# Graph stage: three batches that have only counts move from the end into the middle of the order

## What is computed

```python
edge_index = jnp.stack([src, dst])
x = _layernorm(x + _L0_gnn_ref(x, edge_weight, L0_gnn_bias, edge_index))   # x @ W.T + bias
x = _layernorm(x + _L1_gnn_ref(x, edge_index, ...))   # attention over the edges
x = _layernorm(x + _L2_gnn_ref(x, edge_index, ...))   # GCN: normalised sum over the edges
x = _layernorm(x + _L3_gnn_ref(x, src, dst, ...))     # two SAGE layers: mean over the edges
...
# L0: a dense matrix made from the edges
W = jnp.zeros((OUTDIM, INDIM)).at[row, col].add(nnz_weight)
```

## Time and profile before

| what | us |
|---|---|
| timed runs, median of 3 | 1513.65 |
| lowest and highest of them | 1513.05 and 1515.47 |
| span of the profiled execution | 1553.5 |
| graph stage in the profiled execution, about | 20.5 to 127.6 |

### The profile page before, as it was taken

The page is one execution under the profiler, slowest core; times in us unless marked ns, Lnnn a source line. Parts: engine busy times, 40 slices in busy tenths (PEclk is TensorE's granted clock), DMA queues, the critical chain, the costliest instruction groups (busy, mean ns, idle before and its releaser), DMA issues.

```text
span 1553.5 us, 17781 instructions
## 1 busy us (share of the span) xinstructions
PE 1433.6 (92%) x6845; PEld 1145.2 (74%) x6845; DVE 783.6 (50%) x1359; ACT 421.9 (27%) x716; POOL 254.4 (16%) x309
## 2 busy tenths in 40 slices
PE   3988999748999989899999999999999999999996
PEld 3876888625666656678888888888888888888884
DVE  6996776517888868754336632221033232411243
ACT  7853222235565545312111100110120001201000
POOL 3000000064666655110000010000000100000000
PEclk9997999969999999999999999999999999999998
DMA  1665344454555644152117552230056544400252
GB/s 46 192 181 189 106 126 116 93 157 150 163 155 153 179 146 130 55 185 85 61 42 240 180 189 85 103 145 1 0 190 219 187 124 147 143 1 0 91 194 95
DMA packets 101988, 195.95 MB, mean 126 GB/s; under 512 B 26856, under 2 KB 61465, under 8 KB 101905
## 3 DMA queue, kind: packets, MB, share of 16 engines
q1 hardware_dynamic: 77434, 121.01, 25.8%
q0 software_dynamic: 22800, 73.61, 13.9%
q10 hardware_dynamic: 1670, 0.21, 0.1%
HBM read 140.86 MB, written 53.92 MB: 125 GB/s over the span
## 4 chain that ended last, share of the span: by engine, by line
PE 56%; DVE 1%; DMA 0%; issue 0%; POOL 0%; DVEq 0%; ACT 0%
PE layers_y_ps L1927 35%; PE layers_y_ps L1948 17%; PE layers_turn_ps L1911 2%; PE layers_up_ps L1894 1%; PE layers_y_ps L1964 1%; DMA x_d<-fetched_x 0%; DVE layers_w_lo L2082 0%; DVE layers_y L2126 0%; PE layers_y_ps L1972 0%; DVE layers_y L597 0%; DVE layers_ln_stats L591 0%; PE layers_turn_ps L1882 0%; DVE layers_parts_lo L2099 0%; DVEq L592 0%; PE layers_y_ps L1882 0%
## 5 line engine op out<-in xcount | busy, mean ns | idle before, releaser
L1948 PE MATMUL layers_y_ps<-layers_parts_hi,layers_counts 128*128 128x512 f32 x464 | 143.6, 391 | 0.0
L1948 PE MATMUL layers_y_ps<-layers_parts_lo,layers_counts 128*128 128x512 f32 x464 | 143.3, 390 | 0.0
L1927 PE MATMUL layers_y_ps<-layers_w_hi,layers_parts_hi 128*128 128x512 f32 x400 | 126.0, 396 | 0.0
L1927 PE MATMUL layers_y_ps<-layers_w_lo,layers_parts_hi 128*128 128x512 f32 x400 | 123.6, 390 | 0.0
L1927 PE MATMUL layers_y_ps<-layers_w_hi,layers_parts_lo 128*128 128x512 f32 x400 | 123.5, 390 | 0.0
L509 POOL DMA_INDIRECT attention_got<-xl_d,attention_src x104 | 106.5, 1024 | 63.1 <-DVE attention_weighted L1537 31.3
L1948 PEld LDWEIGHTS layers_y_ps<-layers_parts_lo,layers_counts 128*128 128x128 f32 x464 | 87.1, 188 | 18.7
L1948 PEld LDWEIGHTS layers_y_ps<-layers_parts_hi,layers_counts 128*128 128x128 f32 x464 | 86.9, 188 | 18.9
L1353 PE MATMUL attention_mix_ps<-attention_weighted,attention_hot 128*110 128x260 f32 x368 | 95.7, 384 | 3.7 <-DVE attention_weighted L1537 3.7
L1320 PE MATMUL attention_row_ps<-attention_bent,edges_att_rows 128*128 128x512 f32 x184 | 97.1, 611 | 0.0
L2099 DVE SCALAR_TENSOR_TENSOR layers_parts_lo<-layers_y_ps,layers_parts_hi 128x1024 fp32r<-128x1024 f32 x16 | 19.6, 1225 | 147.5 <-ACT layers_parts_hi L2043 147.5
(11 more groups left out here) (341 smaller groups left out, 2783.4 us busy)
## 6 DMA issues: line engine op xcount, KB each, us to landing
layers_counts<-counts_d SPq DMA_DIRECT2D x30, 640.0 KB, 4.0
layers_rest<-x_d SPq DMA_DIRECT2D x23, 512.0 KB, 4.1
self_d<-layers_y POOLq DMA_DIRECT2D x20, 512.0 KB, 6.0
x_d<-layers_y POOLq DMA_DIRECT2D x19, 512.0 KB, 2.9
fetched_x<-x_d SPq DMA_DIRECT2D x17, 512.0 KB, 3.7
fetched_raw<-in_L_gnn_W_self POOLq DMA_DIRECT2D x16, 512.0 KB, 5.9
fetched_raw<-in_L_gnn_W_neigh POOLq DMA_DIRECT2D x16, 512.0 KB, 9.0
heads_dst_wide<-in_dst_held SPq DMA_DIRECT2D x13, 512.0 KB, 4.0
```

The costliest lines, as they stand in the source:

```text
L1927: last = nc.tensor.matmul(y_ps[n % 2][:, a:a + HALF], rows_in[t][:, k * P:(k + 1) * P], w[k][:, a:a + HALF], start=(k == 0 and p == 0), st ...
L1948: last = nc.tensor.matmul(y_ps[n % 2][:, a:a + HALF], counts[c % 2][:, k, :], part[k][:, a:a + HALF], start=(k == 0 and part is hi), stop= ...
```

## The change

The order of the batches becomes a list. Batch 24 is worked off behind the 6th batch with weights, batch 25 behind the 12th and batch 26 behind the 18th; batches 27 and 28 stay at the end. The order is 0 to 5, 24, 6 to 11, 25, 12 to 17, 26, 18 to 23, 27, 28. All functions take the place `n` in this list and look the batch up as `order[n]`; buffers alternate by place. Counts of turns in the waits for weights become counts of weighted batches so far (`weights_until`). Blocks become whole at other places: blocks of W at places 3, 6, 10, 13, 17, 20, 24, 27, blocks of counts at 3, 6, 10, 13, 17, 20, 24, 27, 27, 29 (they were 3, 6, 9, ... 24 and 3, 6, 9, ... 24, 27, 29). The last two `split_weights` then fall at places 27 and 30, so ACT's loop runs to `BATCHES + 3`. `add_degrees` waits for all earlier readings of degrees, as the sums of the last two pairs now come close together.

```diff
+EARLY_COUNTS, COUNTS_EVERY = 3, 6
...
-    whole_at = [min(-(-(j + 1) * P // (CELL * BATCH)), BATCHES) for j in range(BLOCKS)]
-    pair_at = whole_at[1::2]
-    weights_at = [-(-(k + 1) * P // (CELL * BATCH)) for k in range(KB)]
+    order, unweighted = [], list(range(WEIGHT_BATCHES, BATCHES))
+    for b in range(WEIGHT_BATCHES):
+        order.append(b)
+        if b % COUNTS_EVERY == COUNTS_EVERY - 1 and len(unweighted) > BATCHES - WEIGHT_BATCHES - EARLY_COUNTS:
+            order.append(unweighted.pop(0))
+    order += unweighted
+    weights_until = [sum(b < WEIGHT_BATCHES for b in order[:n]) for n in range(BATCHES + 1)]
+
+    def batches_until(node):
+
+        return 1 + max(n for n, b in enumerate(order) if b * CELL * BATCH < node)
+
+    whole_at = [batches_until((j + 1) * P) for j in range(BLOCKS)]
+    pair_at = [max(whole_at[j:j + 2]) for j in range(0, BLOCKS, 2)]
+    weights_at = [batches_until((k + 1) * P) for k in range(KB)]
     high_at = [at + 3 for at in weights_at]
...
-            for b in range(BATCHES):
+            for n, b in enumerate(order):
                 if b < WEIGHT_BATCHES:
-                    sp.wait_ge(weight_out, b + 1)
-                if b in weights_at:
-                    sp.wait_ge(weight_stored, 16 * b)
+                    sp.wait_ge(weight_out, weights_until[n + 1])
+                if n in weights_at:
+                    sp.wait_ge(weight_stored, 16 * weights_until[n])
...
-                if b in weights_at:
-                    load_weights(weights_at.index(b))
+                if n in weights_at:
+                    load_weights(weights_at.index(n))
                 for j in range(BLOCKS):
-                    if whole_at[j] == b + 1:
-                        sp.wait_ge(added, b + 1)
+                    if whole_at[j] == n + 1:
+                        sp.wait_ge(added, n + 1)
...
-                if 1 <= b <= WEIGHT_BATCHES:
+                if b >= 1 and order[b - 1] < WEIGHT_BATCHES:
                     add_weights(b - 1)
...
-            for b in range(BATCHES):
-                if b < WEIGHT_BATCHES:
-                    weigh_hot(b)
+            for n in range(BATCHES + 3):
+                if n < BATCHES and order[n] < WEIGHT_BATCHES:
+                    weigh_hot(n)
                 for k in range(KB):
-                    if high_at[k] == b:
+                    if high_at[k] == n:
                         split_weights(k)
...
             def add_degrees(pair):
                 pe.wait_ge(added, pair_at[pair])
-                if pair >= 2:
-                    pe.wait_ge(degrees_taken, 2 * (pair - 1))
+                if pair >= 1:
+                    pe.wait_ge(degrees_taken, 2 * pair)
```

More of the change, by code:

```diff
@@ L347, in _, with mark @@
             dve.drain()
-            def mark(hot, held, b, width, ready):
+            def mark(hot, held, n, width, ready):
+                b = order[n]
                 wide = [P, 2 * BATCH, width]
@@ L354, in mark, with mark_sources, mark_keys, add_counts @@
                     ALU.is_equal).then_inc(ready, 1)
[L356 to L367, removed]
+            def mark_sources(n):
+                if n >= 2:
+                    dve.wait_ge(counted, n - 1)
+                    dve.wait_ge(weighted_ready, weights_until[n - 1])
+                mark(src_hot[n % 2], edge_src, n, P, src_ready)
+            def mark_keys(n):
+                if n >= 2:
+                    dve.wait_ge(cells_done, n - 1)
+                mark(key_hot[n % 2], edge_key, n, CELL_COLS, key_ready)
+            def add_counts(n):
+                b = order[n]
                 nodes = slice(b * BATCH * CELL, (b + 1) * BATCH * CELL)
                 held = g["counts_t"][:, :, nodes]
-                dve.wait_ge(counted, b + 1)
-                nc.vector.tensor_tensor(held, count_ps[b % 2][:, :].rearrange("p (n a) -> p a n", a=BLOCKS),
+                dve.wait_ge(counted, n + 1)
+                nc.vector.tensor_tensor(held, count_ps[n % 2][:, :].rearrange("p (n a) -> p a n", a=BLOCKS),
                                         held.bitcast(F32), ALU.add).then_inc(added, 1)
[L374 to L377, removed]
+            def add_weights(n):
+                held = g["weights_held"][0:CELL_COLS, order[n], :]
+                dve.wait_ge(cells_done, n + 1)
+                nc.vector.tensor_tensor(held, weight_ps[n % 2][:, :], held, ALU.add).then_inc(weight_out, 1)
             def take_degrees(pair):
@@ L420, in _, with weigh_hot @@
             act.wait_ge(weight_kept, 1)
[L422 to L426, removed]
+            def weigh_hot(n):
+                b, s = order[n], n % 2
+                act.wait_ge(src_ready, n + 1)
+                if n >= 2:
+                    act.wait_ge(cells_done, n - 1)
                 for t in range(2 * BATCH):
@@ L457, in _, with add_cells @@
                                     g["ident"][0:CELLS, 0:CELLS]).then_inc(weight_turned, 1)
[L459 to L464, removed]
+            def add_cells(n):
+                b, s = order[n], n % 2
+                pe.wait_ge(src_ready, n + 1)
+                pe.wait_ge(key_ready, n + 1)
+                if n >= 2:
+                    pe.wait_ge(added, n - 1)
                 for c in range(BATCH):
@@ L471, in add_cells @@
                 if b < WEIGHT_BATCHES:
-                    pe.wait_ge(weighted_ready, b + 1)
-                    if b >= 2:
-                        pe.wait_ge(weight_out, b - 1)
+                    pe.wait_ge(weighted_ready, weights_until[n + 1])
+                    if n >= 2:
+                        pe.wait_ge(weight_out, weights_until[n - 1])
                     for c in range(BATCH):
@@ L481, in add_cells @@
                 else:
-                    pe.wait_ge(counted, b + 1)
+                    pe.wait_ge(counted, n + 1)
                     pe.sem_inc(cells_done, 1)
```

## The result

| | median us | runs | lowest and highest |
|---|---|---|---|
| before | 1513.27 | 5 | 1512.62 and 1515.47 |
| changed | 1520.6 | 5 | 1519.6 and 1521.42 |

The ratio is 1.0049, with a 95% interval of 1.0038 to 1.006: 7.3 us slower, where +5.1 was forecast and the range ended at 1521.5. The profiled execution of the changed kernel has a span of 1517.8 us. So spans are compared with the second trace, and rows of the graph stage with either.

What follows compares the result with a forecast made beforehand. DVE was taken to set the graph stage's pace, with spare time in the weights' round trip. Terms 0 + 2.9 + 0 + 2.2 = +5.1 us on 1513.65 gave 1518.8 us, range 1515.0 to 1521.5.

Steps and rivals of the forecast that it cites:

- Order of DVE's work: Graph stage turns: same work in either order while DVE is the bound, so moving three turns forward saves 0 us.
- The late round trip: End of graph stage: last weights go through DRAM later, load behind two counts stores, table load uncovered; +2.9 us.
- The gaps: PE idle behind the three early batches: clock falls in two of three, stalling DVE; +2.2 us, bounds 0 and 5.7.
- The next stage: Stage after the graph stage: PE again starts at half clock, 0 us; a high clock would gain at most 1.69 us.
- The sum: Whole kernel: 0 + 2.9 + 0 + 2.2 = +5.1 us, carried over to the median of the timed runs.
- The rival that ends faster: End of graph stage: PE's clock stays up, saving 2.1 us there and 1.7 in the next stage; 1509.9 us, chance 0.06.

Runs made afterwards that it cites:

- the second trace: Both kernels run again unchanged for another trace each: the kernel before 1513.92 us (span 1512.1), the changed kernel 1520.59 us (span 1518.8).
- fill_early: Changed kernel with eight extra matmuls on PE in each of the three early turns without weights; 1516.92 us, ratio to the kernel before 1.0021.
- tail_mended: Changed kernel with the square root's table loaded before the wait for the last weights block, and one counts store issued behind that block's load; 1519.24 us.
- early1: Changed kernel with one early batch without weights in place of three, four staying at the end; 1516.11 us, ratio to the kernel before 1.0008.
- early2: Changed kernel with two early batches without weights in place of three, three staying at the end; 1516.9 us, ratio to the kernel before 1.0021.
- before_fill: Kernel before with eight extra matmuls in each of its five last turns and ten behind the last degrees; 1510.67 us, ratio 0.9982.

## Why the prediction was right, point by point

**Order of DVE's work: right.** Nothing was gained by moving turns. With the clock high (`fill_early`), turn 6 to 27 took 68.5 us where 68.2 was worked out; the 0.3 are in the turn with the third reading of degrees (4.15 us, 3.88 for the second), for a reason that was not looked into.

**The late round trip: right, with its parts.** From the add to the split 10.07 us against 10.0; the whole end 2.7 us (16.0 against 12.7 and the 0.6 of the shorter turns) against 2.9. The load did wait behind the second store, the table load did lose its cover. Moving both showed how little room there is: SP's last store ends only 1 us before DVE in the changed kernel. The prediction had it 0.7 us before (128.7 against 129.4), and covered.

**The gaps: right in kind, sized too small.** The term was 2.2 us, two falls of three, one short and one of middle length. The traces showed stalls of 2.9 us with three falls and 4.1 us with two; the 0.3 us of the turn named above are in both and are not the clock's. A fall that lasts 6.8 us costs 1.9 us (a turn of 5.12 us in place of 3.24), the upper bound that was worked out from 5.9 us of low clock. One of about 3.4 us costs 0.3 to 0.6, less than the 0.8 assumed. The two long falls of the second trace thus make up most of what the term missed. Where the gap had no extra matmuls the clock fell in 10 of 12 gaps: three in the changed kernel, two of three in its second trace, three in `tail_mended`, the one of `early1`, one of two in `early2`. With extra matmuls it fell in none of 6. The rule of the Trainium skill ("TensorE: Matmul & The Clock Gate", "Why this matters for your kernels"), which warns of longer gaps only, does not cover this pattern: PE's idle time was 2.17 us, behind a turn with only 1.07 us of matmuls, and the clock fell.

**The next stage: no gain, nearly.** In the first trace the low clock there was shorter and gave back 1.1 us (DVE's wait 0.53 in place of 1.69); in the second it gave nothing (1.69 again). So what the next stage adds or takes changes from one execution to the next.

**The sum.** In the second traces the stage ends 134.18 - 127.67 = 6.5 us later: 4.1 from the gaps, 2.7 from the end, less 0.2 because turn 6 was that much earlier. The spans differ by 6.7 and those executions' times by 6.7. The 5.1 forecast was 2.2 short against the medians, for the term of the gaps first of all; in the first trace the late start of 1.5 us, which no step had, came on top. The measured 1520.6 lies in the range, but near its end: the range had room for such falls, and the forecast itself took smaller ones.

**The rival that ends faster** had the right price for its parts. A high clock at the end gave 3.0 us between the medians of `before_fill` and the kernel before, against the 3.8 worked out as the most. What it had against it was also right: in the changed kernel the weights are last and hide all of that. In its second trace the last count matmuls ran at the high clock (1.07 us at 122.60, 1.92 in the first trace), and turn 27 to the end was 16.0 us all the same.

## What to carry to other kernels

Turns in another order give the engine that sets the pace the same work: moving some ahead saves nothing by itself and can use up slack elsewhere. Before moving a chain's last producer, count the whole tail that hangs on it, with the queue it enters, the table load that its wait used to hide, and the store that is next in line. And on this kernel an idle gap of 2.17 us on PE, behind a turn with 1.07 us of matmuls, was not free: some cheap matmuls into an unused tile held the clock in 6 of 6 such gaps, and at the end of the kernel before they gained 3.0 us, where the reordering had lost 7.3.

## What the hardware showed that was not expected

The low stretches behind one and the same kind of gap lasted 3.4 to 6.8 us, or did not come at all, and which it is changed from one execution to the next (behind the first early batch 3.4 us in one trace of the changed kernel and none in the other), while two traces of the kernel before agree to 0.1 us on when its clock rises and falls. An issue on SP took longer with two counts stores just issued: the load of a block 1.43 us (124.27) against 0.35 at 111.92. And the first trace's 1553.5 us against 1512.1 shows that one profiled execution can be 41 us longer with an ordinary graph stage; the 41 us arise in the attention stage.
